# Fused four-layer kernel: the cross-attention residual moved ahead of a softmax maximum, and eight per-head weight products issued in pairs

## What is computed

```python
x = x + _L0_xcond_ref(_layernorm(x), cond_1024[:, None, :], ctx_1024, ...)   # self attention, cross attention, GLU
x = x + _L0_ffn_ref(_layernorm(x), ...)                                      # shared expert and top 2 of 7 experts
x = x + _L1_xcond_ref(cond_1024, ctx_1024, _layernorm(x), ...)               # slot attention, three rounds
x = x + _L1_ffn_ref(_layernorm(x), ...)                                      # top 1 of 8 experts
```

```python
h1 = adaln(x, t, norm1_w, norm1_b)
x = mha(h1, h1, attn1_wq, attn1_wk, attn1_wv, attn1_wo, attn1_bo) + x      # 16 heads of 64
h2 = adaln(x, t, norm2_w, norm2_b)
x = mha(h2, context, attn2_wq, attn2_wk, attn2_wv, attn2_wo, attn2_bo) + x # context of 77 rows
h3 = adaln(x, t, norm3_w, norm3_b)
x = glu_ff(h3, ff_w1, ff_b1, ff_w2, ff_b2) + x
```

## Time and profile before

| | |
|---|---|
| time, median of 3 runs | 940.6 us (936.86 to 947.47) |
| time of the profiled execution | 940.69 us |
| its span, first to last instruction | 938.9 us |
| mean granted TensorE clock | 0.904 |
| busy: PE, weight loads, DVE, ACT, POOL | 792.7, 653.7, 566.0, 524.6, 359.9 us |
| iteration 0 | about 22.4 to 50.9 us of the span |
| iterations 3 to 14 | about 116 to 471 us of the span |

### The profile page before, as it was taken

One profiled execution on the slowest core, in us unless ns is written; L12 is line 12 of the kernel. 1 busy time (PEld: TensorE's weight loads), 2 busy tenths in 40 slices (PEclk: granted clock), 3 DMA queues, 4 the chain that ended last, 5 costly groups with the idle time before them and its releaser, 6 DMA issues.

```text
span 938.9 us, 18029 instructions
## 1 busy us (share of the span) xinstructions
PE 792.7 (84%) x5701; PEld 653.7 (70%) x5701; DVE 566.0 (60%) x1941; ACT 524.6 (56%) x1139; POOL 359.9 (38%) x559
## 2 busy tenths in 40 slices
PE   6989899999999999989987588999978777762594
PEld 5866687777877787777775446999746565651593
DVE  1567787776876666776665252333458887885012
ACT  3665566667666666656754132333538988851362
POOL 1233534334333333332346541566512222225463
PEclk9999899999999999999997679999955979785797
DMA  8325305440701510301140041888510000001574
GB/s 257 104 67 154 129 1 163 137 145 25 258 1 36 176 45 18 83 1 34 54 159 26 21 140 27 232 243 256 178 70 1 1 1 1 1 1 34 150 210 132
DMA packets 82055, 88.53 MB, mean 94 GB/s; under 512 B 6155, under 2 KB 69851, under 8 KB 81323
## 3 DMA queue, kind: packets, MB, share of 16 engines
q1 hardware_dynamic: 78475, 80.19, 28.4%
q0 software_dynamic: 3488, 7.20, 2.2%
HBM read 69.03 MB, written 35.17 MB: 111 GB/s over the span
## 4 chain that ended last, share of the span: by engine, by line
PE 58%; DVE 21%; issue 8%; ACT 5%; POOL 4%; SPq 2%; DMA 2%; DVEq 0%; POOLq 0%; ACTq 0%
PE bank L677 8%; PE bank L967 5%; PE bank L683 5%; DVE sb_smax L1473 4%; PE bank L750 3%; PE bank L710 3%; DVE sb_row_sum L1482 3%; PE bank L719 3%; PE bank L975 3%; PE bank L788 2%; DVE sb_st_all L1780 2%; PE bank L1084 2%; PE bank L1076 2%; PE bank L692 2%; PE bank L928 2%
## 5 line engine op out<-in xcount | busy, mean ns | idle before, releaser
L1957 POOL TENSOR_TENSOR sb_expd<-sb_expd,sb_rden 128x512 f32<-128x512 f32 (+1 forms) x128 | 112.2, 877 | 250.0 <-DVE sb_rden L1486 249.8
L1473 DVE TENSOR_REDUCE sb_smax<-bank 128x4 f32<-128x512 f32 (+1 forms) x128 | 74.1, 579 | 75.3 <-PE bank L710 37.9
L2049 POOL TENSOR_TENSOR sb_rstd_all<-sb_rsq_all,sb_halves 128x4 f32<-128x4 f32 x44 | 45.2, 1026 | 130.6 <-DVE sb_rsq_all L1787 130.6
L1196 ACT ACTIVATE sb_expd<-sb_shifted 128x512 f32<-128x512 f32 (+1 forms) x128 | 69.8, 545 | 45.5 <-DVE sb_shifted L1476 44.6
L677 PE MATMUL bank<-sb_h1T,sb_watt 128*128 128x128 f32 x512 | 73.1, 295 | 13.0 <-DVE sb_xb L1462 9.7
L677 PEld LDWEIGHTS bank<-sb_h1T,sb_watt 128*128 128x128 f32 x512 | 66.0, 206 | 18.3 <-DVE sb_xb L1462 10.2
L1482 DVE TENSOR_REDUCE sb_row_sum<-sb_expd 128x4 f32<-128x512 f32 (+1 forms) x128 | 73.0, 570 | 7.9 <-ACT sb_expd L1196 7.8
L1476 DVE TENSOR_TENSOR sb_shifted<-bank,sb_smax 128x512 f32<-128x512 f32 (+1 forms) x128 | 75.0, 586 | 4.4
L967 PE MATMUL bank<-sb_blk_xT,sb_up_w 128*128 128x128 f32 x456 | 57.1, 275 | 0.0
L2015 POOL DMA_INDIRECT back_a<-sb_blk_y,sb_dest_a x38 | 37.0, 973 | 48.8 <-issue 24.9
L967 PEld LDWEIGHTS bank<-sb_blk_xT,sb_up_w 128*128 128x128 f32 x456 | 54.0, 192 | 0.0
(11 more groups left out here) (260 smaller groups left out, 1987.2 us busy)
## 6 DMA issues: line engine op xcount, KB each, us to landing
sb_up_w<-gate_up SPq DMA_DIRECT2D x38, 384.0 KB, 4.2
sb_v<-v_all SPq DMA_DIRECT2D x16, 576.0 KB, 6.6
rows_b<-pad_b SPq DMA_DIRECT2D x7, 1105.0 KB, 10.1
rows_a<-pad_a SPq DMA_DIRECT2D x7, 975.0 KB, 8.3
sb_up_w<-w1b SPq DMA_DIRECT2D x23, 256.0 KB, 3.4
v_all<-sb_moe_w SPq DMA_DIRECT2D x14, 308.0 KB
sb_blk_x<-rows_a SPq DMA_DIRECT2D x38, 65.0 KB, 3.3
sb_picked<-back_a SPq DMA_DIRECT2D x4, 512.0 KB, 5.5
```

Source lines behind the costliest of these rows:

```text
L1196: act.activation(exp_of(i, s, j), shifted[:, u % 2, :, 0:n], ACT.Exp, scale=DH ** -0.5).then_inc(exp_done, 1)
L1473: dve.tensor_reduce(smax[:, u % 2, :], s_in, X, ALU.max).then_inc(max_done, 1)
L1957: pool.tensor_tensor(e, e, rden[:, u % 2, :].unsqueeze(2).broadcast_to([P, QH, n]), ALU.mult).then_inc(norm_done, 1)
L2049: pool.tensor_tensor(rstd_all[:, c], rsq_all[:, 0, c], halves[:, c], ALU.pow).then_inc(root_ready[k], 1)
```

## The change

It has two parts. In `iteration` of VectorE, the wait for `xab_ready` and the call of `residual(i, "wo2", ...)` move from behind the sum of A1 to the front of step 2, ahead of the maximum of A2. The variance of the same rows stays where it was. In iteration 0, the weight products are issued two at a time: a new function takes two banks and issues the matmuls of an even and an odd product alternately, head by head, on partitions 0 to 63 and 64 to 127. For that `FILL` is reordered: `a2_2` goes from the end of step 1 to the end of step 2 and is joined by `a2_3` (from step 3); `b2_0` and `b2_1` (from steps 2 and 3) go to step 4, `b2_2` and `b2_3` to the end of step 5. The order of all other names stays.

```diff
 FILL = [
     ((), ("g2_5",)),
-    (("h2T", "a2_0", "a2_1"), ("a2_2", "wo2", "rank")),
-    (("q1_1", "b2_0", "zT"), ("k1_0",)),
-    (("k1_1", "a2_3"), ("q1_0", "b2_1", "logit")),
-    (("h3T", "b2_2"), ("g2_4",)),
-    (("g2_0", "g2_1", "g2_3"), ("gate", "b2_3")),
+    (("h2T", "a2_0", "a2_1"), ("wo2", "rank")),
+    (("q1_1", "zT"), ("k1_0", "a2_2", "a2_3")),
+    (("k1_1",), ("q1_0", "logit")),
+    (("h3T", "b2_0", "b2_1"), ("g2_4",)),
+    (("g2_0", "g2_1", "g2_3"), ("b2_2", "b2_3", "gate")),
...
+            def head_products(i, kind, first, left, right):
+
+                t = [use(i, f"{kind}_{first + r}") for r in range(2)]
+                for h in range(QH):
+                    for r in range(2):
+                        p, c = slice(DH * r, DH * r + DH), 2 * first + h
+                        mm = pe.matmul(t[r][:, h * P:(h + 1) * P], left[p, c, :], right[p, c, :], start=True, stop=True)
+                        if h == QH - 1:
+                            mm.then_inc(proj_full, 1)
...
-                if name.startswith("a2"):
+                if name in ("a2_0", "a2_2"):
                     if name == "a2_0":
                         pe.wait_ge(ld_att2, 32)
-                    t, j = use(i, name), int(name[-1])
-                    p = slice(DH * (j % 2), DH * (j % 2) + DH)
-                    for h in range(QH):
-                        c = 4 * (j // 2) + h
-                        mm = pe.matmul(t[:, h * P:(h + 1) * P], qk2_w[p, 1, c, :], qk2_w[p, 0, c, :], start=True, stop=True)
-                    mm.then_inc(proj_full, 1)
+                    head_products(i, "a2", int(name[-1]), qk2_w[:, 1, :, :], qk2_w[:, 0, :, :])
...
                 for k in range(N_STEPS):
+                    if k == AT["wo2"] and "C" in S:
+                        dve.wait_ge(xab_ready, c + 1)
+                        residual(i, "wo2", xb[:, :], tile(x0b, c))
                     if scored(k):
                         softmax_in(i, scored(k)[0], scored(k)[2])
                     if summed(k) and k != AT["sums"]:
                         softmax_sums(i, *summed(k))
                     if k == AT["wo2"] and "C" in S:
-                        dve.wait_ge(xab_ready, c + 1)
-                        residual(i, "wo2", xb[:, :], tile(x0b, c))
                         variances("B", c, [(2, xb[:, :], zB, z_ready["B"])])
```

More of the change, by code:

```diff
@@ L764, in fill @@
                     emptied_by([first for first, _ in X_GROUPS].index(i + 1), "hT")
-                if name.startswith("a2"):
+                if name in ("a2_0", "a2_2"):
                     if name == "a2_0":
                         pe.wait_ge(ld_att2, 32)
-                    t, j = use(i, name), int(name[-1])
-                    p = slice(DH * (j % 2), DH * (j % 2) + DH)
-                    for h in range(QH):
-                        c = 4 * (j // 2) + h
-                        mm = pe.matmul(t[:, h * P:(h + 1) * P], qk2_w[p, 1, c, :], qk2_w[p, 0, c, :], start=True, stop=True)
-                    mm.then_inc(proj_full, 1)
-                if name.startswith("b2"):
+                    head_products(i, "a2", int(name[-1]), qk2_w[:, 1, :, :], qk2_w[:, 0, :, :])
+                if name in ("b2_0", "b2_2"):
                     if name == "b2_0":
                         pe.wait_ge(ld_vo2, 32)
[L777 to L782, removed]
+                    head_products(i, "b2", int(name[-1]), vo2_w[:, 0, :, :], vo2_w[:, 1, :, :])
                 if name.startswith("g2"):
```

## The result

The changed kernel takes 928.1 us (median of 6 runs, 926.6 to 931.7); the kernel before, on the same chip, 940.8 us (6 runs, 934.4 to 947.5). The ratio is 0.9875, with a 95% interval of 0.9844 to 0.9906: 1.25% faster. The profiled execution took 928.7 us, its span is 926.9 us, that of before 938.9.

The account below looks back on a forecast made before the run. The prediction took PE to bound the first phase. Moving the residual was to gain 10.3 us and pairing the weight products 0.7 us, 11.0 us off 940.7, so 929.7 us, with a range of 924.4 to 937.

Parts of the forecast that it names:

- The bound and the eleven waits: First phase: PE is the bound; eleven waits of k1_0 for sb_xb go, 0.9 us each, 9.9 us.
- The residual costs nothing on DVE: Iteration 10: idle time before the maximum of A2 hides the moved residual's 0.42 us.
- The expected idle time of 0.1 us or less: Sign: DVE's idle time before the maximum of A2 shrinks to 0.1 us or less.
- D: Rival, chance 0.15: the residual outgrows the idle time, POOL's product comes up to 0.42 us later; 934.1 us.
- What is late next: The transpose of A1 then waits for POOL's product, which limits the gain to 0.97 us an iteration.
- Iteration 13: k1_0 waits for the copy of the ranks, which comes 0.42 us earlier; gain 0.4 us.
- rival B: Rival, chance 0.22: the clock does not fall in iteration 0, 928.0 us; without iteration 13's slow stretch too, 926.3.
- The pairs: Iteration 0: pairing saves PE 2.4 us, a half-clock stretch behind a longer wait costs 1.7; 0.7 us gained.
- the sum: Total gain: 10.3 us from moving the residual plus 0.7 us from the pairs, 11.0 us.
- rival C: Rival, chance 0.12: in iteration 0 ACT's copies bound the pairs, pairing gives nothing, the slow stretch is paid; 932.1 us.
- E, the clock stays low: Rival, chance 0.04: 1.2 GHz lasts from iteration 0's new 1.9 us wait through iteration 1; 953 us.

Follow-up runs that it names:

- The experiment in the second place: The changed kernel with the residual between the subtraction of A2 and the sum of A1: 949.4 us, ratio 0.9946 to the kernel before.

## Why the prediction was right, point by point

**The bound and the eleven waits: right.** PE was the bound, and its idle time came back: 0.87 us an iteration over ten iterations where 0.9 was predicted, 9.5 us over eleven with iteration 14's 0.84 (9.9 predicted).

**The residual costs nothing on DVE: right to 0.08 us.** The predicted start of the transpose of A1, 4.58 us behind the scores (329.36 - 324.78), was 4.66. The expected idle time of 0.1 us or less was wrong, it is 0.32. Of the difference 0.09 us is that the residual starts before the reciprocal ends (317.87 against 317.78 + 0.18 = 317.96), 0.08 that the maximum comes later, and the rest that 0.42 us was taken for the residual where it ends after 0.28: the 0.42 us from its start to the next instruction stood in front of an instruction that reads its result. The experiment in the second place shows 0.31 where the next one does not. This erred on the safe side; D's price of 0.42 us an iteration was too high for the same reason (0.27 us for the later place: 0.31 less most of the 0.08 that the maximum does not lose there).

**What is late next: right.** POOL's product of A1 sets the transpose, and when it was made later (variance in front), the gain went with it.

**Iteration 13: mechanism right, and the rest luck.** 0.4 us was predicted, 1.94 came. What the change does there is to let `k1_0` start 4.69 us behind the scores instead of 5.02, 0.33 us; the other 1.6 us (3.62 - 2.02) is the slow stretch that wasn't there this time. The prediction had it as an addition to rival B, priced 1.7. It comes and goes: behind a wait of 1.89 or 1.90 us the 16 records of `k1_0` and `k1_1` took 2.02 us in after and in the kernel with the residual alone, but 3.40 us when the changed kernel ran again and 3.14 with the pair repeated. With the order of before they took 3.62 us in before and 3.61 with the repeats of iterations 1 and 2, but 2.02 with the pairs alone. So it isn't the change that takes the stretch away.

**The pairs: right.** 16 records in 1.16 us, a 1.93 us wait, a slow stretch behind it, 0.75 us gained where 0.7 was predicted; without the slow stretch 2.3 where 2.4 was predicted, at a price of 1.6 where 1.7 was. The 2.3 are 2.1 us of PE's work and the 0.24 us wait; the 0.14 us wait at `v2_0`, foreseen as 0.2 and left out of the sum, is the missing tenth. On the other chips the wait that goes was 0.83 and 1.48 us, so there the pairs would bring more than the sum has. ACT kept up, so rival C is out. By the rule of the Trainium skill ("TensorEngine Tiling (Array Packing)", Performance Considerations) that the emptying of PSUM may become the bound, the gain would have been zero. The page says so of a fourfold speedup, and a pair is a twofold one; here the measurement doesn't bear it out: ACT copies a pair's two banks in 1.09 us, and PE was busy for 10.40 of 10.40 us.

**E, the clock stays low: did not happen** in iteration 0, where the granted clock is 1.00 again from 30.60 us. A small form of it did, in iteration 15: its wait of 2.17 us was there before too (2.09), but 1.2 GHz lasted longer, and 1.29 us of the gain were lost up to the last `wo2` (46.13 us from the second scores of iteration 15, 44.84 before). The sum had no term for that. It seems to go with the move: on the other chips this way takes 43.2 and 43.6 us in the two kernels with DVE's old order, and 44.8 to 46.4 in the six that have the residual further ahead and repeat nothing in iteration 15. But 44.8 is in both groups once before is counted, and how the move would bring it about is open. So the total, 940.69 - 928.74 = 12.0 us between the profiled executions, is near the 11.0 predicted partly by luck, because three things that weren't in the sum, +0.84 at the start, +1.5 in iteration 13 and -1.3 behind iteration 15, came out at +1.1 together.

What stays open is what decides between full and half clock behind a wait of 1.9 us, and why in the total the repeats in iteration 0 are not seen: their 1.6 us were lost to a lower granted clock behind iteration 15 in the one trace there is.

## What to carry to other kernels

A matmul that waits for a bank is served by moving the one instruction that frees it into idle time of the emptying engine, and it pays per iteration only as far as the next reader's chain (here POOL's product) allows; look for that limit first, and leave the rest of the work (here the variance, 0.63 us an iteration) where it is. Products on two halves of the array are paired by alternating matmul by matmul. Before work is taken away ahead of a wait that another engine ends, see what the longer wait does to the clock; here the kernel that computes something again in such waits was 8.6 us faster, three quarters of what the change itself gave, of which 5.9 us show in iterations 0 to 3, where most of the repeats stand.

## What the runs showed of the hardware that was not expected

- Repeated matmuls whose results are thrown away made the kernel faster: 943.4 to 934.8 us. Behind waits of 0.95 to 1.06 us left in iterations 0 to 2 no half clock was seen; behind those of 1.79 us and more in the same iterations it was in 30 of the 32 cases that the traces have, and behind the wait of 1.89 or 1.90 us in iteration 13 in 3 of 7.
- Often, not always: with the same products in iteration 0, the wait of 1.93 us was followed by a slow stretch in after, and by none in the kernel with the residual in the second place, where the way from the second scores of iteration 0 to those of iteration 1 took 26.16 us, not 27.75. The other exception is the wait of 2.00 us in iteration 1 of the kernel with the residual alone. The rows with the residual in the second place:

```profile
25.17 1.16 PE L710 MATMUL bank<-sb_k1T,sb_q1T 64*128 64x128 f32 x16 [1.93 <-DVE sb_shifted L1476]
26.27 1.16 PE L677 MATMUL bank<-sb_h1T,sb_watt 128*128 128x128 f32 x8
```

- Two sets of four matmuls on the two halves of the array, one set after the other, take 1.64 us: not 2.2 as apart, and not 1.10 as alternating.
- The same kernel takes 940.8 us on one chip and 953.7 to 954.8 on others, which is as much as the change is worth; the difference lies behind the first phase: the changed kernel starts its last `wo2` at 508.28 us on the first chip and at 507.63 where it ran again, and its spans are 926.9 and 941.4 us.
